# A causal attention pipeline with probability buffers four deep instead of three, and two kinds of copies issued by ScalarE instead of SyncE

## The reference

```python
c_q = x @ W_DQ;  c_kv = x @ W_DKV                # latent width 256
Q = [c_q @ W_UQ | rope(c_q @ W_QR)]              # 16 heads, 64 + 32 wide
K = [c_kv @ W_UK | rope(x @ W_KR)]               # the 32 rope columns are shared by all heads
V = c_kv @ W_UV
scores = clip(Q @ K.T, -80, 80), causal mask
attn = softmax(scores / sqrt(96)) @ V
x = layernorm(x + attn @ W_O)
h = gelu(x @ Wq_fc.T + b_fc + lora_fc)           # Wq: weights rounded to 8 bits, one scale per matrix
x = layernorm(x + h @ Wq_proj.T + b_proj + lora_proj)
```

## Time and profile before

| | us |
|---|---|
| median of 2 runs | 2297.44 (2297.27 to 2297.6) |
| the profiled execution | 2298.96 |
| its span, first to last instruction, slowest core | 2297.3 |
| spans of the eight cores | 2282.9 to 2297.3 |
| phases 0 and 1 | up to about 244 |
| phase 2 with the first production | about 244 to 965 |
| the rest | about 965 to 2297 |

### The profile page before, as it was taken

One profiled execution on the slowest core, in us unless ns is written; L12 is line 12 of the kernel. 1 busy time (PEld: TensorE's weight loads), 2 busy tenths in 40 slices (PEclk: granted clock), 3 DMA queues, 4 the chain that ended last, 5 costly groups with the idle time before them and its releaser, 6 DMA issues.

```text
span 2297.3 us, 28286 instructions; the slowest of 8 cores (2282.9 to 2297.3 us)
## 1 busy us (share of the span) xinstructions
PE 1386.1 (60%) x7038; PEld 689.8 (30%) x7038; DVE 1061.2 (46%) x1381; ACT 844.8 (37%) x1165; POOL 83.5 (4%) x136
## 2 busy tenths in 40 slices
PE   1073666666766666544443233323888898798885
PEld 0020122222222222111110011112565575565654
DVE  2257677777677777664445734443101201112012
ACT  0000255555555555413354035553324324233241
POOL 0000000000000000000000000000000000000000
PEclk9575877778777787657755565556899898898987
DMA  5500012111111113322221022231000000000000
GB/s 183 153 5 0 12 55 63 47 58 61 48 58 44 63 42 97 115 67 79 72 65 33 1 65 83 83 89 54 19 1 20 19 1 19 4 17 19 1 19 19
DMA packets 49661, 112.28 MB, mean 49 GB/s; under 512 B 12528, under 2 KB 23280, under 8 KB 47200
## 3 DMA queue, kind: packets, MB, share of 16 engines
q0 software_dynamic: 14912, 54.53, 7.6%
q1 hardware_dynamic: 24800, 34.96, 5.2%
q10 hardware_dynamic: 9792, 20.98, 3.0%
HBM read 97.47 MB, written 8.39 MB: 46 GB/s over the span
## 4 chain that ended last, share of the span: by engine, by line
PE 37%; DVE 25%; ACT 16%; DMA 12%; issue 7%; DVEq 1%; ACTq 1%; SPq 0%; POOLq 0%
PE PSD L314 29%; DVE CL L674 7%; ACT PT L680 4%; ACT QSG L781 4%; DMA QSG<-wFCr 4%; DMA QSG<-wPRr 4%; DVE MXW L546 3%; PE PSD L658 3%; PE BIG L588 2%; PE PS L314 2%; DVE KH L509 2%; DVE CL L667 2%; ACT QTI L785 2%; DMA STG<-xT 1%; ACT TSQ L1159 1%
## 5 line engine op out<-in xcount | busy, mean ns | idle before, releaser
L680 ACT ACTIVATE PT<-CL 128x1024 bf16<-128x1024 f16 (+1 forms) x320 | 310.7, 971 | 305.7 <-DVE CL L667 134.4
L314 PE MATMUL PSD<-XT,RTF 128*128 128x256 bf16 x2048 | 308.0, 300 | 122.8 <-ACT HH L1107 120.8
L658 PE MATMUL PSD<-QH,KH 96*128 96x512 bf16 (+3 forms) x640 | 227.5, 447 | 96.6 <-DVE CL L667 90.0
L674 DVE TENSOR_SCALAR CL<-PSD 128x1024 f16<-128x1024 f32 x192 | 235.0, 1224 | 90.5 <-PE BIG L588 58.7
L314 PE MATMUL PSD<-HH,RTP 128*128 128x256 bf16 x2048 | 237.3, 275 | 53.1 <-DVE UPt L1124 53.1
L588 PE MATMUL BIG<-PT,VP 128*65 128x512 bf16 (+3 forms) x640 | 217.3, 428 | 71.4 <-ACT PT L680 70.2
L314 PEld LDWEIGHTS PSD<-XT,RTF 128*128 128x128 bf16 x2048 | 195.5, 105 | 196.8 <-issue 140.3
L314 PEld LDWEIGHTS PSD<-HH,RTP 128*128 128x128 bf16 x2048 | 196.5, 98 | 85.1 <-issue 55.1
L1107 ACT ACTIVATE HH<-PSD,BFCS,SML 128x256 bf16<-128x256 f32 x256 | 144.3, 564 | 143.5 <-PE PSD L314 132.0
L781 ACT ACTIVATE QSG<-QSG,SML 128x512 f32<-128x512 f32 x128 | 104.0, 813 | 214.7 <-DMA QSG<-wPRr 70.9
L588 PEld LDWEIGHTS BIG<-PT,VP 128*65 128x65 bf16 x640 | 81.9, 130 | 210.0 <-issue 192.3
(11 more groups left out here) (148 smaller groups left out, 1341.0 us busy)
## 6 DMA issues: line engine op xcount, KB each, us to landing
STG<-wFCr POOLq DMA_DIRECT2D x32, 512.0 KB, 4.4
STG<-wPRr POOLq DMA_DIRECT2D x32, 512.0 KB, 4.3
STG<-xT SPq DMA_DIRECT2D x8, 1024.0 KB, 6.2
QSG<-wFCr POOLq DMA_DIRECT2D x32, 256.0 KB, 3.0
QSG<-wFCr ACTq DMA_DIRECT2D x32, 256.0 KB, 2.8
QSG<-wPRr POOLq DMA_DIRECT2D x32, 256.0 KB, 3.1
QSG<-wPRr ACTq DMA_DIRECT2D x32, 256.0 KB, 2.7
out<-OST SPq DMA_DIRECT2D x64, 128.0 KB, 1.9
```

What stands on the lines that cost most here:

```text
L314: e.matmul(outap, la, ra, start=st, stop=sp),
L658: e.matmul(self.PSD[pslot][:, 512 * half: 512 * half + qext], self.KHB[b][0:96, 128 * kt:128 * kt + 128], self.QHB[b][0:96, qlo:qlo + qext ...
L674: e.tensor_scalar(self.CLB[cs][:, 0:qw], self.PSD[pslot][:, 0:qw], 80.0, -80.0, ALU.min, ALU.max),
L680: etok = P.s(lambda e, cs=cs, qw=qw: e.activation(self.PTB[cs][:, 0:qw], self.CLB[cs][:, 0:qw], AF.Exp, scale=ISQ), waits=[ctok, self.pv_t ...
```

## The change

CL and PT get four buffers instead of three, and every wait that goes with a buffer's reuse is moved from three pairs to four. `pend` may hold 6 tiles instead of 4, so PV runs three pairs behind the scores. The rope copies to QH (16) and KH (2) are issued by ScalarE's queue instead of SyncE's, at the same places of the emission order and with the same waits.

```diff
-        self.CLB = [A.alloc("CL%d" % i, [128, 1024], F16, 2, 2) for i in range(3)]
-        self.PTB = [A.alloc("PT%d" % i, [128, 1024], BF16, 2, 2) for i in range(3)]
+        self.CLB = [A.alloc("CL%d" % i, [128, 1024], F16, 2, 2) for i in range(4)]
+        self.PTB = [A.alloc("PT%d" % i, [128, 1024], BF16, 2, 2) for i in range(4)]
...
         def qr_step():
             def go():
-                prod["qr"] = P.d("sync", "dqr", lambda e, h=h, b=b: e.dma_start(
+                prod["qr"] = P.d("scalar", "dqr", lambda e, h=h, b=b: e.dma_start(
...
-        self.krk = [P.d("sync", "dqr", lambda e, b=b: e.dma_start(
+        self.krk = [P.d("scalar", "dqr", lambda e, b=b: e.dma_start(
...
-                cs = pj % 3
+                cs = pj % 4
...
-                               waits=[stok, exp_pair.get(pj - 3)])
+                               waits=[stok, exp_pair.get(pj - 4)])
...
-                    waits=[ctok, self.pv_tok.get(2 * pj - 5)])
+                    waits=[ctok, self.pv_tok.get(2 * pj - 7)])
...
-                while len(pend) > 4:
+                while len(pend) > 6:
                     emit_pv(pend.pop(0))
```

More of the change, by code:

```diff
@@ L670, in phase2 @@
                                    self.TRI[:, 0:qw], ALU.max, ALU.min),
-                               waits=[stok, exp_pair.get(pj - 3), self.tri_r])
+                               waits=[stok, exp_pair.get(pj - 4), self.tri_r])
                 else:
```

## The result

| | before | after |
|---|---|---|
| median, us | 2298.96 | 2276.20 |
| ratio with its 95% interval | | 0.9884 [0.9855, 0.9914] |
| spans of the eight cores | 2282.9 to 2297.3 | 2262.3 to 2275.3 |
| mean granted clock of TensorE | 0.751 | 0.762 |

The change takes 22.8 us, where 2287 and a gain of 10 us against the profiled span were forecast. The result lies inside the stated range; the forecast gain was less than half of the measured one. Some executions of every kernel are slower, at a lower granted clock: the medians in this document count them and the ratios leave them out, so a ratio isn't the quotient of the two medians beside it. In the profiled executions the mean of the eight spans falls by 21.6 us, all of it in phase 2.

What follows compares the result with a forecast made beforehand. VectorE, with the most work in the attention stage, was taken as the bound. Heads 0 to 14 -9.8, mid-head +1.4, head 15 -2.0, DMA issues +0.2 sum to -10.2 us from 2297.3: forecast 2287, range 2262 to 2303.

Runs made afterwards that it cites:

- one kernel: The kernel before with four buffers, PV two pairs behind the scores in pairs 0 to 9 and three from pair 10 on; ratio 0.9979.
- 36 of another: The changed kernel itself: four buffers, PV three pairs behind the scores, rope copies on ScalarE's queue; 2276.20 us, ratio 0.9884.
- filled kernel before: The kernel before with 12 extra unused matmuls ahead of pair 2 and of pair 12 in each head; 2268.18 us, ratio 0.9854.

## What to carry to other kernels

Deepening a software pipeline pays where an in-order engine stops behind an item that is not yet needed; find that place in the timeline first, as here a 0.58 us copy ahead of another, which could be moved without a buffer. Ask next what makes the idle stretches themselves: spreading reductions that stood in twos ahead of critical work brought some three times what the deeper pipeline did (63 us of 2273). And a sum made at one clock holds only if the change leaves the clock alone.

## Not expected of the hardware

TensorE's clock was worth more than the reordering, though VectorE has the most work in the stage: 24 unused matmuls a head, in time in which PE waited anyway, raised the granted clock in 300 to 800 us from 0.77 to 0.94, took 2.17 us from a head where the lag took 1.32, and 1.5% from the kernel. With the same order of matmuls behind the same idle stretch, the clock was already low at PE's restart in 101 of 112 heads of one kernel and in 36 of another, and the part behind it took 19.00 and 18.69 us.

This is the filled kernel before in 300 to 800 us:

```profile
300.00:800.00 500.00, 353.56 (x1397) 132.23 (x1421) 385.95 (x379) 283.01 (x331) 34.67 (x48) 0.94 0.19 56
```
